# The token stage of a vision tower, reordered: statistics three units ahead, column mean and bias row by VectorE, loads in another order

## The reference, cut to what matters

```python
def tok(img):                                   # 64 images, 3 x 96 x 96
    x = patches(img)                            # (64, 36, 768): 6 x 6 patches
    x = layernorm(x, ln1_g, ln1_b)              # over 768
    x = x @ W_lin + b_lin                       # (64, 36, 192)
    x = layernorm(x, ln2_g, ln2_b)              # over 192
    return concat([cls, x], 1) + pos_embedding  # (64, 37, 192)

h = tok(x)
h = h + attention(layernorm(h))     # 8 heads, relative positions, Wo and bo
h = h + experts(layernorm(h))       # top 2 of 8, capacity limited
```

## Time and profile before

| | us |
|---|---|
| median of 3 runs | 620.72 (619.73 to 621.04) |
| the profiled execution | 620.7 |
| its span, from first to last instruction | 618.9 |
| busy PE / DVE / ACT / POOL | 542.4 / 433.4 / 258.8 / 218.2 |
| mean granted TensorE clock, share of full | 0.939 |

### The profile page before, as it was taken

How to read it: one execution, slowest core, us unless ns; L and a number is a source line. 1 busy time by engine, 2 the same in 40 slices (tenths; PEclk the granted TensorE clock), 3 DMA queues, 4 the chain that set the end, 5 groups by cost and what they waited for, 6 DMA issues and landing times.

```text
span 618.9 us, 12396 instructions
## 1 busy us (share of the span) xinstructions
PE 542.4 (88%) x4284; PEld 503.6 (81%) x4284; DVE 433.4 (70%) x1008; ACT 258.8 (42%) x415; POOL 218.2 (35%) x206
## 2 busy tenths in 40 slices
PE   4998477999999999999999796667999999999983
PEld 4997377989989999899899673344899999999982
DVE  6669676476776776777867757662778777777853
ACT  1333333242542443434425205402765685595560
POOL 0247320112012021021120105018587787787364
PEclk9999788799999999999999757869999999999997
DMA  8978632201202102112012008505375475466250
GB/s 198 227 170 246 171 80 63 46 14 39 51 0 51 34 16 51 26 25 51 11 39 51 2 4 226 141 1 134 82 165 134 94 170 136 92 145 149 21 166 32
DMA packets 61978, 54.96 MB, mean 89 GB/s; under 512 B 29174, under 2 KB 52534, under 8 KB 61152
## 3 DMA queue, kind: packets, MB, share of 16 engines
q1 hardware_dynamic: 52799, 46.04, 29.4%
q0 software_dynamic: 9152, 8.59, 8.3%
HBM read 39.32 MB, written 18.27 MB: 93 GB/s over the span
## 4 chain that ended last, share of the span: by engine, by line
PE 44%; DVE 13%; ACT 12%; issue 10%; SPq 9%; DMA 5%; POOL 3%; DVEq 2%; POOLq 0%; ACTq 0%
PE PS L1035 7%; PE PS L726 6%; PE PS L749 6%; ACT wide L1077 4%; PE PS L705 4%; PE PS L1033 4%; ACT hTh L1219 3%; PE PS L733 2%; DVE hTl L1686 2%; PE PS L742 2%; PE PS L740 2%; PE PS L741 2%; PE PS L1010 2%; SPq L496 2%; ACT b2w L1225 2%
## 5 line engine op out<-in xcount | busy, mean ns | idle before, releaser
L1737 POOL TENSOR_TENSOR rs<-ve,nhalf 111x1 f32<-111x1 f32 (+2 forms) x37 | 24.7, 668 | 276.4 <-DVE ve L1333 197.3
L1867 POOL DMA_INDIRECT running_sums<-ye,gid x42 | 73.4, 1747 | 34.8 <-DVE ye L1710 25.6
L1035 PE MATMUL PS<-w2hl,hTh 128*128 128x384 f32 (+1 forms) x288 | 82.8, 357 | 0.0
L1033 PE MATMUL PS<-w2hl,hTl 128*128 128x192 f32 (+1 forms) x288 | 73.5, 255 | 4.0 <-DVE hTl L1686 4.0
L1841 POOL DMA_INDIRECT xe<-routed_rows,gid x48 | 53.3, 1111 | 42.7 <-DVE gid L1651 28.5
L1010 PE MATMUL PS<-xeT,w1h 128*128 128x370 f32 x288 | 64.2, 331 | 2.1 <-issue 1.4
L1686 DVE TENSOR_TENSOR hTl<-hf,hTh 128x740 fp32r<-128x740 f32 x48 | 44.6, 928 | 24.7 <-ACT hTh L1219 23.5
L1033 PEld LDWEIGHTS PS<-w2hl,hTl 128*128 128x128 f32 (+1 forms) x288 | 53.7, 186 | 6.4 <-issue 5.6
L705 PE MATMUL PS<-xT,wh 128*128 128x222 f32 x264 | 46.8, 287 | 7.7 <-DVE xT L1347 7.7
L1035 PEld LDWEIGHTS PS<-w2hl,hTh 128*128 128x128 f32 (+1 forms) x288 | 52.9, 184 | 0.5
L1010 PEld LDWEIGHTS PS<-xeT,w1h 128*128 128x128 f32 x288 | 50.4, 188 | 2.8 <-issue 1.8
(11 more groups left out here) (241 smaller groups left out, 1288.0 us busy)
## 6 DMA issues: line engine op xcount, KB each, us to landing
wide<-x SPq DMA_DIRECT2D x24, 288.0 KB, 13.3
w1r<-L_ffn_W SPq DMA_DIRECT2D x16, 384.0 KB, 4.9
rel_scores<-wide SPq DMA_DIRECT2D x66, 73.0 KB
w2r<-L_ffn_W SPq DMA_DIRECT2D x8, 576.0 KB, 4.6
w1r<-L_ffn_W SPq DMA_DIRECT2D x16, 192.0 KB, 4.5
wide<-rel_scores SPq DMA_DIRECT2D x22, 111.0 KB, 2.3
out<-running_sums SPq DMA_DIRECT2D x1, 1776.0 KB, 7.6
h_tokens<-narrow SPq DMA_DIRECT2D x24, 72.0 KB, 1.9
```

The source lines that it names most:

```text
L1033: pe.matmul(PS[0:n, bank, 0:D], hTl[:, c, at], w2hl[:, c, 0, :], start=(c == 0), stop=False, skip_group_check=True)
L1035: last = pe.matmul(PS[0:n, bank, 0:2 * D], hTh[:, c, at], both(w2hl[:, c, :, :]), start=False, stop=(c == HC - 1), skip_group_check=True)
L1867: p_.indirect_dma_start(sums, at, ye[0:r, e % 2, n, :], None, bounds_check=B * T + NT * 128 - 1, oob_is_err=True, compute_op=ALU.add).then ...
```

## The change

VectorE's statistics run three units ahead, and their end and the power on GpSimd come per chunk (three units). The column mean is one product of the matrix of 1/768 with a sum over the six weight blocks that VectorE makes; the bias row is likewise one product with a sum made by VectorE, behind the first unit's product. SP issues the thirteen constants ahead of x chunks 3 to 5, stores chunks 0 and 1 ahead of the Q and K weights and chunk 2 ahead of the V weights, loads groups 0 and 1 alone, then 2 to 9, and sends the scores of step 0 ahead of the last chunk's store, the other groups and the zeros. The output weights have a semaphore of their own, and their high and low part move behind step 0. ScalarE's high parts of the Q, K and V weights move to the last two units and behind them.

```diff
-N_EARLY, N_CONST, N_QKV, N_AW = 5, 16, 12, 14
+N_EARLY, N_CONST, N_QKV, N_AW = 5, 16, 12, 13
...
-            load_x(3)
-            load_x(4)
-            load_x(5)
...
-            sp.wait_ge(s_tT, 3 * NH // 2)
-            sp.wait_ge(s_v1, 2)
-            at = 0
-            for W in (Wq, Wk, Wv):
+            def load_qkv(W, at):
...
-                at += n
+
+            sp.wait_ge(s_set, 1)
+            sp.dma_start(h_dram[B * T:ROWS, :], zeros[0:ROWS - B * T, 0:D]).then_inc(s_ho[0], 16)
...
-            sp.wait_ge(s_set, 1)
-            sp.dma_start(h_dram[B * T:ROWS, :], zeros[0:ROWS - B * T, 0:D]).then_inc(s_ho[0], 16)
-            for q in range(CHUNKS // 2):
+            for q in range(2):
...
+            sp.wait_ge(s_tT, 7)
+            sp.wait_ge(s_v1, 3)
+            load_qkv(Wq, 0)
+            load_qkv(Wk, H * K)
+            sp.wait_ge(s_ht, 3)
+            store_rows(2)
+            load_qkv(Wv, 2 * H * K)
...
-            load_rows(0, GROUPS_A)
+            load_rows(0, 2)
...
-            sp.dma_start(wo[:, :, :], Wo.rearrange("(c p) d -> p c d", p=128)).then_inc(s_aw, 16)
-            sp.dma_start(sums[B * T:B * T + NT * 128].rearrange("(p n) d -> p n d", p=128),
-                         bc(zeros[:, :].rearrange("p (a d) -> p a d", a=1), [128, NT, D])).then_inc(s_h2, 16)
+            load_rows(2, GROUPS_A)
+            sp.wait_ge(s_h, 64)
+            sp.dma_start(wo[:, :, :], Wo.rearrange("(c p) d -> p c d", p=128)).then_inc(s_wo, 16)
...
-            sp.wait_ge(s_ht_last, 1)
-            store_rows(CHUNKS - 1)
-            sp.wait_ge(s_ho[1], 16 * 4 * CHUNKS // 2)
-            load_rows(GROUPS_A, NG)
...
+            sp.wait_ge(s_ht_last, 1)
+            store_rows(CHUNKS - 1)
+            sp.wait_ge(s_ho[1], 16 * 4 * CHUNKS // 2)
+            load_rows(GROUPS_A, NG)
+            sp.dma_start(sums[B * T:B * T + NT * 128].rearrange("(p n) d -> p n d", p=128),
+                         bc(zeros[:, :].rearrange("p (a d) -> p a d", a=1), [128, NT, D])).then_inc(s_h2, 16)
...
-            for c in range(PC):
-                last = pe.matmul(PS[:, 6, 0:D], meanw[:, :], W_cen[:, c, :], start=(c == 0), stop=(c == PC - 1))
-            last.then_inc(s_mean, 1)
+            pe.matmul(PS[:, 6, 0:D], meanw[:, :], wsum[:, :], start=True, stop=True).then_inc(s_mean, 1)
...
-            for c in range(PC):
-                pe.matmul(PS[:, 7, 0:D], bc(bb1[:, c:c + 1], [128, 128]), W_raw[:, c, :], start=(c == 0), stop=False)
-            pe.matmul(PS[:, 7, 0:D], ones[0:1, :], blin[:, :], start=False, stop=True).then_inc(s_brow, 1)
...
-
+                if u == 0:
+                    pe.wait_ge(s_gw, 2)
+                    pe.matmul(PS[:, 7, 0:D], ones[:, :], wb1[:, :], start=True, stop=False)
+                    pe.matmul(PS[:, 7, 0:D], ones[0:1, :], blin[:, :], start=False, stop=True).then_inc(s_brow, 1)
...
+            def qkv_high(n):
+                act.wait_ge(s_qkv, 16 * N_QKV)
+                a, z = QKV_PIECES[n]
+                nc.scalar.copy(wh[:, :, a:z], wraw[:, :, a:z]).then_inc(s_wh, 1)
+
...
-                if u >= UNITS - NF:
-                    if u == UNITS - NF:
-                        act.wait_ge(s_qkv, 16 * N_QKV)
-                    a, z = QKV_PIECES[u - (UNITS - NF)]
-                    nc.scalar.copy(wh[:, :, a:z], wraw[:, :, a:z]).then_inc(s_wh, 1)
+                if u in (UNITS - 2, UNITS - 1):
+                    n = u - (UNITS - 2)
+                    qkv_high(n)
...
-            a, z = QKV_PIECES[NF]
-            nc.scalar.copy(wh[:, :, a:z], wraw[:, :, a:z]).then_inc(s_wh, 1)
+            qkv_high(2)
+            qkv_high(3)
...
-            nc.scalar.copy(woh[:, :, :], wo[:, :, :]).then_inc(s_woh, 1)
...
+            act.wait_ge(s_wo, 16)
+            nc.scalar.copy(woh[:, :, :], wo[:, :, :]).then_inc(s_woh, 1)
...
-            last.then_inc(s_gw, 1)
-            dve.wait_ge(s_gw, 1)
-
-            def ln1_stats(j, w):
-
-                if w % (NH // 2) == 0:
-                    dve.wait_ge(s_x[j][w // (NH // 2)], 64)
+            ch(last)
+            v.tensor_reduce(wsum[:, :], W_cen[:, :, :].rearrange("p c d -> p d c"), AX.X, ALU.add).then_inc(s_gw, 1)
+            ch(v.tensor_scalar(wb1[:, :], W_raw[:, 0, :], bb1[:, 0:1], None, ALU.mult))
+
+            def ln1_stats(u):
+
+                j, w = u // NH, u % NH
+                if w % NF == 0:
+                    dve.wait_ge(s_x[j][w // NF], 64)
...
-            def ln1_end(j):
+            def ln1_end(q):
+                j, ws = q // 2, slice(q % 2 * NF, q % 2 * NF + NF)
...
-                for w in range(NH):
+                for w in range(ws.start, ws.stop):
...
-                v.tensor_scalar(ve1[:, j, :], mv1[:, j, :, 1], EPS, None, ALU.add).then_inc(s_v1, 1)
+                v.tensor_scalar(ve1[:, j, ws], mv1[:, j, ws, 1], EPS, None, ALU.add).then_inc(s_v1, 1)
...
-            for w in range(NH):
-                ln1_stats(0, w)
+            for c in range(1, PC):
+                ins = v.scalar_tensor_tensor(wb1[:, :], W_raw[:, c, :], bb1[:, c:c + 1], wb1[:, :], ALU.mult, ALU.add)
+                if c < PC - 1:
+                    ch(ins)
+            ins.then_inc(s_gw, 1)
+            for u in range(NF):
+                ln1_stats(u)
...
-            for j in range(NH // 2):
-                dve.wait_ge(s_r1, j + 1)
-                for w in range(NH):
-                    u = j * NH + w
-                    dve.wait_ge(s_tz, u + 1)
-                    v.scalar_tensor_tensor(zt[:, j, w, :], PS[:, 4 + u % 4, 0:D], rs1[:, j, w:w + 1], cB[:, :],
-                                           ALU.mult, ALU.add).then_inc(s_tze, 1)
-
-                    if j + 1 < NH // 2:
-                        ln1_stats(j + 1, w)
-                        if w == NH - 1:
-                            ln1_end(j + 1)
-                    if w % NF == NF - 1:
-                        ln2_stats(j, w // NF)
-                    if w % NF == 1 and u >= NF:
-                        ln2_rows((u - NF) // NH, (u - NF) // NF % 2)
-                    if u == UNITS - 3:
-                        dve.wait_ge(s_h, 32)
-                        ln1_var(0)
-                    if u == UNITS - 2:
-                        ln1_rows(0)
-                        qkv_low(0)
-                    if u == UNITS - 1:
-                        qkv_low(1)
+            for u in range(UNITS):
+                j, w = u // NH, u % NH
+                q = u // NF
+                if u % NF == 0:
+                    dve.wait_ge(s_r1, q + 1)
+                dve.wait_ge(s_tz, u + 1)
+                v.scalar_tensor_tensor(zt[:, j, w, :], PS[:, 4 + u % 4, 0:D], rs1[:, j, w:w + 1], cB[:, :],
+                                       ALU.mult, ALU.add).then_inc(s_tze, 1)
+                if q + 1 < CHUNKS:
+                    if u % NF == 0:
+                        ln1_stats(u + 3)
+                        ln1_stats(u + 4)
+                    if u % NF == 1:
+                        ln1_stats(u + 4)
+                        ln1_end(q + 1)
+                if u % NF == 1 and q > 0:
+                    ln2_rows((q - 1) // 2, (q - 1) % 2)
+                if u % NF == 2 and u < UNITS - 1:
+                    ln2_stats(q // 2, q % 2)
+                if u == UNITS - 3:
+                    dve.wait_ge(s_h, 32)
+                    ln1_var(0)
+                if u == UNITS - 2:
+                    ln1_rows(0)
+                    qkv_low(0)
+            qkv_low(1)
...
+            ln2_stats(NH // 2 - 1, 1)
...
             dve.wait_ge(s_aw, 16 * N_AW)
+            dve.wait_ge(s_h, 64)
+            step(0)
             dve.wait_ge(s_woh, 1)
             v.tensor_tensor(wol[:, :, :], wo[:, :, :], woh[:, :, :].bitcast(F32), ALU.subtract).then_inc(s_wol, 1)
-            step(0)
-            dve.wait_ge(s_h, 64)
             v.tensor_copy(upperb[:, :], upper[:, :])
...
-            def rstd1(j):
-                pool.wait_ge(s_v1, j + 1)
-                rsqrt(rs1[:, j, :], ve1[:, j, :]).then_inc(s_r1, 1)
+            def rstd1(q):
+                pool.wait_ge(s_v1, q + 1)
+                ws = slice(q % 2 * NF, q % 2 * NF + NF)
+                rsqrt(rs1[:, q // 2, ws], ve1[:, q // 2, ws]).then_inc(s_r1, 1)
...
+            rstd1(1)
...
-            rstd1(1)
+            rstd1(2)
...
+            rstd1(3)
...
+            rstd1(4)
...
-            rstd1(2)
...
+            rstd1(5)
```

More of the change, by code:

```diff
@@ L285, in build @@
         zt = piece(128, UNITS * D).rearrange("p (j w d) -> p j w d", j=NH // 2, w=NH)
+        wsum = piece(128, D)
+        wb1 = piece(128, D)
         clsB = piece(64, 2 * D).rearrange("p (a d) -> p a d", a=2)
@@ L506, in _ @@
             sp.dma_start(tok[:, :], c_tok).then_inc(s_aw, 16)
+            load_x(3)
+            load_x(4)
+            load_x(5)
             hv = h_dram[0:B * T, :].rearrange("(b t) d -> b t d", t=T)
@@ L844, in step @@
                         pe.wait_ge(s_v[0], s + 1)
+                        if is_step(s, 1) and g == 0:
```

(3 more changed lines are left out.)

3 lines of the change are left out of this document (1 added, 2 removed).

## The result

The changed kernel takes 613.16 us (median of 4 runs, 611.56 to 613.43) against 620.27 (619.73 to 621.04) of the kernel before on the same chip: a ratio of 0.9878, 95% interval 0.9861 to 0.9894, 7.1 us less. The profiled execution is the fastest of the four, 611.56 us with a span of 609.7; the other spans are 611.1 to 611.6.

The account below looks back on a forecast made before the run. The bound was taken as token-stage waits: SP held at constants, VectorE waiting for chunk 3, and the row hand-over. Gains 1.4 + 3.55 + 1.45 + 0.1 = 6.5 off 620.7 gave 614.2 us, range 608.3 to 618.5.

Parts of the forecast that it names:

- The place: Token stage and hand-over: the steady loop begins sooner, itself untouched; granted clock 0.50 in step 1 as before.
- Start: worth nothing: Column mean and bias row: product 0 about 2 us sooner, nothing on the path, since chunk 3 decides next.
- Constants ahead: chunk 3 five us later, 39.5: SP's queue: thirteen constants ahead of x delay chunk 3 by 5 us, from 34.46 to 39.5.
- the constants cost little: Rival on SP's queue: constants cost 1.5 us, VectorE hardly waits, path 3.5 us shorter, 610.7; chance 0.13.
- a rival for x: SP held at the constants in front of x3: chunk 3 lands at 46, clock falls, 622.7; chance 0.07.
- Third chunk at 55.0, groups issued at 59.2, there at 63.3: Hand-over: third chunk of rows finished 1.4 us earlier, first two groups there 4.95 us earlier than 68.25.
- The stretch from chunk 3 to the third chunk: VectorE 10.7 us to chunk 2's normalisation, 4.0 to GpSimd's end, 0.8 for GpSimd's roots: 39.5 to 55.0.
- The landing of 4.1: Hand-over: the first two groups land 4.1 us after issue, between bounds of 1.3 and 6.46.
- First transposed rows 9.55 behind it: From first groups to first projection: 9.55 us instead of 10.97, the last chunk's second statistics (1.42) moved behind.
- First softmax 2.9 us behind the second transposed rows, without a wait for the scores: Step 0 to 1: transposed rows at 89.0, softmax at 91.9; the old 2.07 us wait for scores goes.
- the rival's event: Token stage: TensorE idles 2 to 3 us before unit 9, clock falls, 3 to 4 us lost, 617.7; chance 0.10.
- The clock stays up in step 1: Rival: TensorE's gap closes, step 1 takes like step 2, 5.5 us less, 608.7; chance 0.17.

Follow-up runs that it names:

- run with x first: The changed kernel with x chunks 3 to 5 back ahead of the thirteen constants; 617.22 us, ratio 0.9941 to the kernel before.
- the lead alone: The kernel before with only VectorE's statistics three units ahead instead of six; 620.44 us, ratio 0.9988 to the kernel before.
- the hand-over alone: The kernel before plus new store and weight order, two groups first, scores ahead, VectorE's two moves, ScalarE's later high parts; 618.52 us, ratio 0.9960.
- the run with the statistics ahead: The changed kernel with the last chunk's second statistics back ahead of the first transposed rows; 616.09 us, ratio 0.9916 to the kernel before.
- the run with the constants between: The changed kernel with x chunks 3 to 5 first and the constants between the stores of chunks 0 and 1; 615.18 us, ratio 0.9910.
- the last run: The changed kernel with wol, index operations and GpSimd's chunk 4 finish later, x before constants, SP's queue laid out anew; 602.97 us, ratio 0.9694.
- the run with the finish later: The changed kernel with GpSimd finishing chunk 4 only behind the first transposed rows; 612.39 us, ratio 0.9869 to the kernel before.

## Why the prediction was right, and where not

**The place** was right: the loop of steps begins earlier and is itself unchanged, and the granted clock in step 1 is 0.50 as before. 614.2 was forecast and 613.16 measured. That it came so close is in part luck: one edit was booked with the wrong sign, and two terms were wrong in opposite directions, as said below.

**Start: worth nothing.** It held inside the trace; that undoing it came out 2.1 us worse, with intervals that just touch, stays open. The reduction took 2.09 us (I took 1.6, bounds 0.8 to 3), product 1 came at 19.18, and VectorE waits at unit 6 with either start. Product 0 took 3.52 us, others 2.12, at a granted clock of 1.00 in 14 to 18; so it was not "at half clock", as an expectation says, and what slowed it no row shows.

**Constants ahead: chunk 3 five us later, 39.5.** The size is 2.6 us in the profiled execution (37.06) and 2.8 to 4.8 in the seven other traces; the bounds of 1.5 us and of a landing at 46 held. The rival "the constants cost little" (1.5 us, VectorE hardly waits) is not it, but the profiled 2.6 is nearer to it than to the five: by the prediction's own sign, a wait to about 39.5, chunk 3 came 2.4 us too soon there. But the prediction booked this edit as a pure loss: if the constants cost only their bytes, it said, the sum would give 3.5 us more gain. The run with x first has no delay at all and is 3.9 us slower than the changed kernel. This is the step that failed. What I had read in the earlier trace rows, that SP is held at these constants with the weights and stores behind it, was in the account of the bound and as a rival for x, but not in the sum as what the edit takes away. The sum still came out, because its terms were positions (finished at 55.0, stored at once) that silently took SP to be free.

The parts by ratio show how they lean on each other: the lead alone gives 0.7 us (not clear of nothing), the hand-over alone 2.5, lead, hand-over and start together 3.7 (the run with x first), and the order of the constants another 3.9. The lead makes the third chunk ready and the constants' place makes SP ready; the lead without that place waits for SP. The constants' place without the lead was not run.

**Third chunk at 55.0, groups issued at 59.2, there at 63.3.** 52.88, 57.10 and 61.71 in the profiled execution, each about 2 us sooner, which is chunk 3 again: in the run with the statistics ahead, chunk 3 at 39.15, they are 54.97, 59.02 and 64.80 (the last with a landing of 5.3). That the other three runs of the changed kernel have a later chunk 3 as well would explain their 2 us; they have no trace, so this is argued and not shown.

The stretch from chunk 3 to the third chunk was forecast at 15.5 us and takes 15.82, but not as summed. To the normalisation of chunk 2 it takes 11.8 us, not 10.7: the end of the second statistics, an operation on 3 elements a partition, takes 1.38 us at 43.48, beside GpSimd's multiplication at 43.44, where the same operation took 0.17 at 25.74. From there on it takes 4.0 us, as in the kernel before; the 0.8 for GpSimd's roots did not come on top.

**The landing of 4.1** was 4.12 from the second issue, and 4.0 to 5.8 in the other traces with two groups. **First transposed rows 9.55 behind it**: 9.45, and 1.54 more with the statistics put back.

**First softmax 2.9 us behind the second transposed rows, without a wait for the scores**: 2.97, and a wait of 2.02 with the scores put back.

**The rivals.** In the profiled execution the clock did not fall in the token stage: it is 1.00 from 34 to 60, and TensorE stood only 0.44 us for chunk 3. It did fall where chunk 3 came at 38.69 to 39.27, in four of the eight traces: TensorE stood 1.95 to 3.05 us there, and its granted clock was 0.50 for some 3 us behind that. TensorE's timeline and a window (columns as above) of the run with the statistics ahead:

```profile
39.17 0.87 PE L670 MATMUL PS<-ident,wide 128*128 128x128 f32 x6 [2.40 <-DMA wide<-x]
...
40.00:42.00 2.00, 2.00 (x8) 2.00 (x7) 2.00 (x6) 0.80 (x1) 0.00 (x0) 0.50 1.03 221
```

So the rival's event came, and its price did not: these four too take 15.8 us from chunk 3 to the third chunk, where it had 3 to 4 us more. TensorE's slower products are not what that stretch waits for. SP did not stand in front of x long enough to matter (7.2 us in all at the two constants). "The clock stays up in step 1" was the rival with most behind it: it did not come by this change, but once 2.6 us of VectorE's work were out of the way of the softmax, it came.

## What to carry to other kernels

Moving a transfer in a queue moves two things, its landing and everything behind it on the queue that issues it; put both into the sum, and look for the wait that takes the place of the one you remove. Where two engines hand work over, ready times on both sides have to move together, so undo one part at a time from the full change as well as trying each part alone. Ahead of a stretch in which TensorE has little to do, look for work on another engine that could stand behind it: a gap that closes there can give back the clock as well.

## What the runs showed of the hardware

**How long SP is held at a small transfer depends on what lies ahead of it, not on the transfer alone.** The same constant, `pos_f`, held SP 12.01 us with the loads of x in front in the kernel before, 10.52 in the run with x first, 4.52 in the changed kernel, 3.69 behind the store of chunk 0 in the run with the constants between, and 0.40 in the last run. In the last run the constant `ind`, which stands directly ahead of it in all the others, had moved behind it as well; which of the transfers ahead holds SP no run separates.

**VectorE and GpSimd shut each other out on some operations.** In the changed kernel the normalisation of rows takes 1.75 us beside GpSimd's multiplication and 0.67 without, the low part of 64 partitions 1.80 and 0.69; GpSimd's own operation beside the latter takes 1.83 us where others of its form take 1.40. With GpSimd held back in the run with the finish later, VectorE's two are short again (0.67 and 0.69). The Trainium skill, page "SBUF — State Buffer", section "Who interferes with whom", says that the two share a port pair as an exclusive lock, which a VectorE operation with two inputs in SBUF or in a two-port mode contends for, the later one waiting for the whole instruction of the other. The trace agrees.

**The landing of a load can differ by 2.2 us between executions** whose programs are alike up to there, but for the start of one (37.06 to 39.27 for chunk 3). This shifts the rest of the token stage, and a single profile can lie at either end of it.
